# The last expert layer of a four-layer tower: all experts over all tokens, or chosen pairs gathered into blocks

## The chip, the core and the metric

The kernel runs on one core of one Trainium2 chip. The metric is the device time of one execution in microseconds. Engines are named as in the profile: PE (TensorE), PEld (its weight loads), DVE (VectorE), ACT (ScalarE), POOL (GpSimd), SP (SyncE, which here only issues DMAs). "SPq" or "ACTq" rows are DMA issues.

## The reference, cut to what matters

The program is a language-model tower of four layers over 2 x 1024 tokens of width 128, in float32. Each layer is an attention part and a feed-forward part, each behind a layernorm and added to h. Two of the feed-forward parts are mixtures of experts that pick two experts per token: the one of layer 1 (8 experts, hidden width 512) and the one of layer 3 (16 experts of hidden width 96, and a shared one that every token passes). Layer 3's is

```python
g = jnp.clip(h[..., ::2], -gate_clamp, gate_clamp)
u = jnp.clip(h[..., 1::2], -up_clamp, up_clamp)
swiglu5 = g * jax.nn.sigmoid(g * alpha) * gate_scale * (u + up_shift)
...
h = xf @ shared_w1 + shared_b1
z = swiglu5(h, *shared_act) @ shared_w2 + shared_b2
w, idx = jax.lax.top_k(softmax(xf @ gate_w + gate_b), 2)      # w is then divided by its sum
cw = sum over the two of one_hot(idx, 16) * w
he = einsum('nd,edh->enh', xf, expert_w1) + expert_b1
oe = einsum('enh,ehd->end', swiglu5(he, *expert_act[e]), expert_w2) + expert_b2
y = einsum('ne,end->nd', cw, oe)                              # y + z is added to h
```

All but two of the 16 weights in a row of `cw` are zero, so an expert's result counts only for the tokens that picked it.

## The kernel before

The stages run one after another, each in one or more blocks; at a block's end all engines meet. `h` stays in SBUF as 16 tiles of 128 tokens. In a block the order on each engine is written out by hand, and semaphores join the engines. An opening block of a stage, one that only issues loads, holds all engines until SP has issued them.

**Layer 1's heads** (`l1_heads`, attention) keep PE, ACT, DVE and POOL at work; SP has nothing to do there.

**Layer 1's experts** (`stage_l1_ffn`, `slots`, `l1_experts`) already work on chosen pairs. An opening block clears a scratch tensor in DRAM for each batch row (`rows_dram`, 23 blocks of 128 rows each) and loads all second weights `w2_all` (2 MB) and small tables, `b1_all` among them. Two layernorms and the router follow. `slots` counts, for each expert, the tokens that picked it, rounds each count up to whole blocks of 128, and gives each pair of token and pick a slot, and each block an owner (its expert). In `l1_experts`, POOL scatters the rows of the 16 token tiles, twice for two picks, to their slots with indirect DMAs of 64 KB. For each block SP reads the owner into a register and loads its first weights (`load`), and loads the block's rows (`rows`); PE turns the rows, ACT copies them, PE, DVE, ACT and PE do the two products, and ACT issues the store of the results to DRAM. POOL gathers them back when a batch row is complete, and `combine` adds them to `h` by their shares on DVE. The 16 gathers of the second batch row stand behind everything.

**Layer 3's experts** (`stage_l3_ffn`, `l3_expert_scalars`, `l3_experts`) run every expert over every token: 17 experts times 4 units of 512 tokens make 68 units. For a unit PE makes gate and up (`up`), ACT copies each with its bias (`fetch`), DVE limits each (`clip`, L2472), ACT takes the sigmoid, POOL multiplies twice (L2456, L2458), PE makes the second product (`down`, L2388), and DVE adds it to `h` by the token's weight for this expert (`add`, L2482), which is zero for most. The loop over experts is a real loop with two experts a turn.

Of the kernel before, what the change touches and what calls it, by code (L numbers as in the profile page):

```python
# [12 lines left out]
F32 = mybir.dt.float32  # L13
I32 = mybir.dt.int32
# [4 lines left out]
P = 128  # L19
# [101 lines left out]
def layernorm(nc, m, name, src, dst, dstT, gain=None, shift=None, loaded=None):  # L121

    with ExitStack() as ctx:
# [397 lines left out]
def stage_l1_attn(nc, m, w):  # L521
    layernorm(nc, m, "ln_l1a", m.h, m.xn, m.xnT)
    with ExitStack() as ctx:
# [11 lines left out]
        l1_heads(nc, m, r)  # L535
# [126 lines left out]
def l1_heads(nc, m, r):  # L662
# [4 lines left out]
    with ExitStack() as ctx:  # L667
# [23 lines left out]
        block = ctx.enter_context(nc.Block())  # L691

# [412 lines left out]
def l1_experts(nc, m, r):  # L1105
# [5 lines left out]
    with ExitStack() as ctx:  # L1111
# [59 lines left out]
        def _(pool):  # L1171
# [19 lines left out]
            pool.wait_ge(r.w2_in, 48)  # L1191
# [17 lines left out]
        def _(pe):  # L1209
# [31 lines left out]
            pe.wait_ge(r.w2_in, 48)  # L1241
# [99 lines left out]
def stage_l1_ffn(nc, m, w):  # L1341
    with ExitStack() as ctx:
# [3 lines left out]
        r = Core()  # L1346
# [4 lines left out]
        r.b_r, r.ln_g, r.ln_b = sb("b_r", [1, 8]), sb("ln_g", [P, 1]), sb("ln_b", [P, 1])  # L1351
        r.b2_dram, r.b1_dram, r.W1_dram, r.W2_dram = w["L1_ffn_b2"], w["L1_ffn_b1"], w["L1_ffn_W1"], w["L1_ffn_W2"]
        r.s_router, r.n_router = signals(nc, m, "l1f_")("router"), 48
        r.rows_dram = [nc.dram_tensor(f"l1f_rows{b}", (L1_BLOCKS * P, D), F32).ap() for b in range(B)]
        r.s_cleared, zeroed = signals(nc, m, "l1f_")("cleared"), signals(nc, m, "l1f_")("zeroed")
        zero = sb("zero", [P, D])
        r.w2_all, r.b1_all, r.b2 = sb("w2_all", [P, 8, 4 * D]), sb("b1_all", [P, 8, 4]), sb("b2", [8, D])
        r.w2_in = signals(nc, m, "l1f_")("w2_in")
        with nc.Block() as block:
            @block.gpsimd  # L1360
            def _(pool):
                pool.memset(zero[:, :], 0.0).then_inc(zeroed, 1)

            @block.sync
            def _(sp):
                sp.dma_start(r.b_r[:, :], row(w["L1_ffn_b_r"])).then_inc(r.s_router, 16)
                sp.dma_start(r.ln_g[:, :], col(w["L1_ffn_ln_g"]), allow_slow_non_contiguous=True).then_inc(r.s_router, 16)
                sp.dma_start(r.ln_b[:, :], col(w["L1_ffn_ln_b"]), allow_slow_non_contiguous=True).then_inc(r.s_router, 16)
                sp.wait_ge(zeroed, 1)
                for b in range(B):  # L1370
# [1309 lines left out]
```

## Time and profile before

| | us |
|---|---|
| median of 3 runs | 1763.08 (1761.98 to 1763.42) |
| the profiled execution | 1766.68, its span 1764.7 |
| layer 1's heads | 134.9 to 421.8 |
| layer 1's experts, first layernorm to last combine | 439.7 to 624.5 |
| layer 3's experts, first layernorm to last add | 1512.9 to 1757.8 |
| its loop, first POOL multiply to last add | 1557.2 to 1757.8 |

Busy shares of the span: PE 79%, DVE 73%, ACT 45%, POOL 47%. The DMA engines move 37.2 MB, most of it in layer 1's experts. A row of a timeline begins with its start and the time from there to the end of the instructions merged in it, in us; in brackets stands how long the engine was idle before, and what ended that. PEclk is the granted clock of TensorE as a share of 2.4 GHz; 0.50 is its lower level, 1.2 GHz.

### The profile page before, as it was taken

Reading aid. Unit: us, or ns where it says so; the run is one execution under the profiler, and the core shown is the slowest. Engines: PE = TensorE matmul, PEld = TensorE weight load, DVE = VectorE, ACT = ScalarE, POOL = GpSimd, SP = SyncE. Lnnn points to the kernel's source line nnn. Section 1 sums busy time; section 2 is a strip of 40 time slices with the busy share of each in tenths; the row PEclk is TensorE's granted clock in tenths of the full one; section 3 lists DMA queues with packets and bytes.
Section 4 is the critical chain, followed back from the end, with each engine's and each line's share of the span. In section 5 each row is a group of like instructions: output and inputs, shape, how many; then the busy total and the mean of one; then the engine's idle time right before and its main releaser. Section 6 shows DMA issues by size and latency. Waiting matters only on the chain. (4 is left out here: it accounts for less than half of the span.)

```text
span 1764.7 us, 30850 instructions
## 1 busy us (share of the span) xinstructions
PE 1386.9 (79%) x10352; PEld 941.4 (53%) x10360; DVE 1282.3 (73%) x2404; ACT 802.9 (45%) x1006; POOL 821.1 (47%) x624
## 2 busy tenths in 40 slices
PE   2775899994369522258999999999999996499997
PEld 1552666663359511144567666666666664355554
DVE  4265465552625459744699999999999994579997
ACT  2232434441125211014566666666766661166664
POOL 2021333230276656212355555555555542169997
PEclk9986999997579865558999999999999998699998
DMA  3000000003158400000000000000000000000000
GB/s 113 1 1 1 2 2 3 2 2 110 15 145 229 122 6 0 0 0 1 1 1 1 0 0 0 0 0 0 0 0 0 0 1 0 6 13 13 11 12 29
DMA packets 45967, 37.20 MB, mean 21 GB/s; under 512 B 11100, under 2 KB 37367, under 8 KB 45623
## 3 DMA queue, kind: packets, MB, share of 16 engines
q1 hardware_dynamic: 36102, 28.28, 5.9%
q0 software_dynamic: 2048, 4.20, 0.8%
q10 hardware_dynamic: 7728, 3.55, 0.7%
q8 instruction: 56, 0.92, 0.2%
q14 instruction: 33, 0.26, 0.1%
HBM read 26.83 MB, written 9.18 MB: 20 GB/s over the span
## 5 line engine op out<-in xcount | busy, mean ns | idle before, releaser
L1914 POOL TENSOR_TENSOR ta_ex<-ta_ex,ta_left 128x1024 f32<-128x1024 f32 x128 | 302.6, 2364 | 317.2 <-ACT ta_left L1867 316.5
L1826 PEld LDWEIGHTS ta_ps_o<-ta_exT,ta_vseq 128*32 128x32 f32 x2048 | 213.2, 110 | 101.9 <-ACT ta_exT L1859 88.2
L1777 PE MATMUL ta_ps_s<-ta_kT,ta_qz 128*128 (+1 forms) x512 | 242.5, 596 | 20.8 <-ACT ta_ex L1855 20.0
L1826 PE MATMUL ta_ps_o<-ta_exT,ta_vseq 128*32 128x128 f32 x2048 | 247.6, 274 | 6.4 <-ACT ta_exT L1859 6.4
L1859 ACT ACTIVATE ta_exT<-ta_ps_t 128x1024 f32<-128x1024 f32 x128 | 131.1, 1024 | 142.4 <-PE ta_ps_t L1806 142.4
L1932 DVE MAX8 ta_top<-ta_ps_s 128x8 f32<-128x1024 f32 x128 | 156.7, 1224 | 46.2 <-PE ta_ps_s L1777 46.0
L1939 DVE MATCH_REPLACE8 ta_left<-ta_top,ta_ps_s 128x1024 f32<-128x1024 f32 x128 | 155.2, 1212 | 0.0
L1944 DVE MAX8 ta_top<-ta_left 128x8 f32<-128x1024 f32 x128 | 154.5, 1207 | 0.0
L1949 DVE MATCH_REPLACE8 ta_left<-ta_top,ta_left 128x1024 f32<-128x1024 f32 x128 | 154.5, 1207 | 0.0
L1855 ACT ACTIVATE ta_ex<-ta_ps_s,ta_ntop 128x1024 f32<-128x1024 f32 x128 | 142.3, 1111 | 23.8 <-DVE ta_left L1939 23.1
L1867 ACT ACTIVATE ta_left<-ta_left,ta_ntop 128x1024 f32<-128x1024 f32 x128 | 147.0, 1149 | 1.4
L1806 PE MATMUL ta_ps_t<-consts,ta_ex 128*128 128x128 f32 x1024 | 137.8, 278 | 0.8 <-POOL ta_ex L1914 0.8
L1777 PEld LDWEIGHTS ta_ps_s<-ta_kT,ta_qz 128*128 128x128 f32 x512 | 87.3, 190 | 88.0 <-issue 74.4
L1806 PEld LDWEIGHTS ta_ps_t<-consts,ta_ex 128*128 128x128 f32 x1024 | 111.6, 141 | 22.0 <-issue 18.6
L946 ACT ACTIVATE l1h_score<-l1h_work 128x2048 f32<-128x2048 f32 (+1 forms) x40 | 68.5, 1711 | 111.3 <-PE l1h_work L820 111.3
L2456 POOL TENSOR_TENSOR l3e_sig<-l3e_gate,l3e_sig 96x512 f32<-96x512 f32 x68 | 98.7, 1452 | 37.3 <-ACT l3e_sig L2434 37.3
L2388 PEld LDWEIGHTS l3e_ps_d<-l3e_w,l3e_te 96*128 96x128 f32 x544 | 67.4, 195 | 62.7 <-issue 58.3
L2472 DVE TENSOR_SCALAR l3e_gate<-l3e_gate,l3f_limit 96x512 f32<-96x512 f32 x68 | 99.1, 1458 | 0.0
L2458 POOL TENSOR_TENSOR l3e_te<-l3e_up,l3e_sig 96x512 f32<-96x512 f32 x68 | 95.7, 1408 | 5.3
L1016 POOL TENSOR_TENSOR l1h_faded<-l1h_qk,l1h_fade 128x256 f32<-128x256 f32 (+1 forms) x80 | 67.1, 878 | 55.0 <-ACT l1h_fade L959 47.4
L2388 PE MATMUL l3e_ps_d<-l3e_w,l3e_te 96*128 96x128 f32 x544 | 80.2, 292 | 7.1 <-POOL l3e_te L2458 4.8
L841 PE MATMUL l1h_y<-l1h_score,l_v 128*32 128x128 f32 (+1 forms) x1536 | 81.8, 330 | 3.4 <-issue 3.4
(563 smaller groups left out, 2511.9 us busy)
## 6 DMA issues: line engine op xcount, KB each, us to landing
l1e_w<-in_L_ffn_W_dram SPq DMA_DIRECT2D x46, 256.0 KB
l1f_rows<-l1f_zero SPq DMA_DIRECT2D x2, 1472.0 KB, 9.3
l1e_x<-l1f_rows SPq DMA_DIRECT2D x46, 64.0 KB
l1e_outs<-l1e_y ACTq DMA_DIRECT2D x46, 64.0 KB
l3e_w<-in_L_ffn_expert_w_dram SPq DMA_DIRECT2D x16, 96.0 KB, 1.9
ids<-in_x_dram SPq DMA_DIRECT2D x1, 1024.0 KB
consts<-in_consts_dram SPq DMA_DIRECT2D x1, 1024.0 KB, 5.5
out_dram<-h SPq DMA_DIRECT2D x1, 1024.0 KB, 6.1
```

Of the source, the lines that this page charges most:

```text
L1777: ins = pe.matmul(ps_s[:, i % 2, half * BANK:(half + 1) * BANK], qz[:, odd, h, :], kT[:, grp, bass.ds(at.key0[i // PAIR] + half * BANK, BA ...
L1806: ins = pe.transpose(ps_t[:, j * P:(j + 1) * P], ex[:, i % 4, j * P:(j + 1) * P], m.ident)
L1826: ins = pe.matmul(ps_o[a:a + 2 * TW, grp * P:(grp + 1) * P], vseq[:, j, h, :], exT[:, i % 2, j, :], start=(j == 0), stop=(j == CH - 1))
L1855: act.activation(ex[:, i % 4, :], ps_s[:, i % 2, :], ACT.Exp, bias=ntop[:, i % 4:i % 4 + 1], scale=SC).then_inc(s_free, 1)
L1859: act.activation(exT[:, i % 2, :, :].rearrange("p j q -> p (j q)"), ps_t[:, :], ACT.Copy).then_inc(exT_in, 1)
L1867: act.activation(left[:, i % 4, :], left[:, i % 4, :], ACT.Exp, bias=ntop[:, i % 4:i % 4 + 1], scale=SC).then_inc(left_exp, 1)
L1914: pool.tensor_tensor(ex[:, i % 4, :], ex[:, i % 4, :], left[:, i % 4, :], ALU.subtract).then_inc(kept, 1)
L1932: dve.max(top[:, i % 2, 0, :], ps_s[:, i % 2, :]).then_inc(max_done[0], 1)
L1939: dve.match_replace(left[:, i % 4, :], top[:, i % 2, 0, :], ps_s[:, i % 2, :], -BIG).then_inc(first_out, 1)
L1944: dve.max(top[:, i % 2, 1, :], left[:, i % 4, :]).then_inc(max_done[1], 1)
L1949: dve.match_replace(left[:, i % 4, :], top[:, i % 2, 1, :], left[:, i % 4, :], -BIG).then_inc(left_ready, 1)
L2388: ins = pe.matmul(ps_d[:, u % 2, t * P:(t + 1) * P], te[:, g, t * P:(t + 1) * P], w2[:, k, :], start=True, stop=True)
```

## The change

Layer 3's experts get the form of layer 1's. `slots` is run for 16 experts and 32 blocks per batch row. `l3_experts` works on pairs of 128-row tiles: 8 pairs for the shared expert, straight from the turned tokens, then 32 pairs of gathered blocks. First and second weights of an expert are packed beforehand into one DRAM tensor, so that a block has one weight load, into one of 16 buffers. The six scalars and two biases of each block's expert come from seven small matmuls with a table of owners (`hot`) into `par`. The limits are now taken on DVE straight from PSUM (one pass that adds the bias and takes the minimum, one in SBUF that takes the maximum; for up the maximum is fused with the product), and POOL keeps one multiply per pair. Hidden buffers are three deep (`LAG`), the row buffers four.

The clearing of both layers' scratch rows, the packing, and layer 1's small tables are issued by SP in the heads' block; `w2_all` and layer 3's tables are issued by SP inside the layernorm's block (`fetch`), and both opening blocks are gone.

```diff
-        l1_heads(nc, m, r)
+        early = [l1_ffn_early(nc, m, w), l3_early(nc, m, w)]
...
+        l1_heads(nc, m, r, issue_early)
...
+        block.sync(early)
...
-        with nc.Block() as block:
-            @block.gpsimd
-            def _(pool):
-                pool.memset(zero[:, :], 0.0).then_inc(zeroed, 1)
...
-        layernorm(nc, m, "ln_l1f", m.h, m.xn, None)
+        layernorm(nc, m, "ln_l1f", m.h, m.xn, None, fetch=fetch)
...
+        slots(nc, m, r, "l3k", L3_E, L3_BLOCKS, r.raw_act[:, 0:L3_E, 1])
...
+    SHARED, PAIRS = TILES // 2, TILES // 2 + B * NB // 2
+    STAGES, LAG = 16, 3
...
+            def load(j):
+                for n in blocks(j):
+                    s, e = n % STAGES, sp.value_load(r.owner[0:1, n // NB, n % NB:n % NB + 1], min_val=0, max_val=E - 1)
+                    if n >= STAGES:
+                        sp.wait_ge(down_ready, SHARED + (n - STAGES) // 2 + 1)
+                    sp.dma_start(packed[:, s, :], m.packed_dram[bass.ds(e, 1), :, :].rearrange("e p f -> p (e f)")).then_inc(staged[s], 16)
+
+            def rows(j):
+                q = j - SHARED
+                b, n = q // (NB // 2), 2 * (q % (NB // 2))
+                if n == 0:
+                    sp.wait_ge(scattered[b], 16 * 2 * CH)
+                if q >= 4:
+                    sp.wait_ge(x_turned, q - 3)
+                sp.dma_start(x[:, q % 4, :, :], r.rows_dram[b][n * P:(n + 2) * P, :].rearrange("(k p) d -> p k d", k=2)).then_inc(x_in[q % 4], 16)
...
+            for j in range(SHARED, PAIRS):
+                if j + 3 < PAIRS:
+                    rows(j + 3)
+                    load(j + 3)
...
+            def swish(j):
+                pool.wait_ge(sig_ready, j + 1)
+                pool.tensor_tensor(sig[:, j % LAG, :, :], gate[:, j % LAG, :, :], sig[:, j % LAG, :, :], ALU.mult).then_inc(t1_ready, 1)
...
+            for j in range(SHARED):
+                if j < 4:
+                    for t, k in jobs[4 * j:4 * j + 4]:
+                        scatter(0, t, k)
+                swish(j)
+            for j in range(SHARED, SHARED + NB // 2):
+                swish(j)
+                for t, k in jobs[3 * (j - SHARED) // 2:3 * (j - SHARED + 1) // 2]:
+                    scatter(1, t, k)
+            for j in range(SHARED + NB // 2, PAIRS):
+                swish(j)
+                i = j - SHARED - NB // 2 - 3
...
+                if i >= 0:
+                    for t, k in jobs[5 * i // 4:5 * (i + 1) // 4]:
+                        gather(0, t, k)
...
+            for j in range(PAIRS):
+                if j + 3 < PAIRS:
+                    up(j + 3)
+                down(j)
+                if SHARED <= j + 4 < PAIRS:
+                    turn(j + 4)
...
+            def keep(j):
+                q = j - SHARED
+                act.wait_ge(down_ready, j + 1)
+                if q >= 4:
+                    act.wait_ge(y_out[q % 4], 16 * (q // 4))
+                act.activation(y[:, q % 4, :, :], ps_d[:, j % 2, 0:2 * P].rearrange("p (k d) -> p k d", k=2), ACT.Copy).then_inc(y_ready, 1)
...
+            for j in range(PAIRS):
+                sigmoid(j)
+                if SHARED <= j + 3 < PAIRS:
+                    flip(j + 3)
+                if j - 1 >= SHARED:
+                    keep(j - 1)
...
+            def clip(j):
+                dve.wait_ge(up_ready, j + 1)
+                if j >= LAG:
+                    dve.wait_ge(t1_ready, j - LAG + 1)
+                    dve.wait_ge(te_ready, j - LAG + 1)
+                for k in range(2):
+                    p = weights(j, k)[2]
+                    h = ps_h[0:L3_I, j % 2, 2 * k * P:(2 * k + 2) * P]
+                    dve.tensor_scalar(gate[:, j % LAG, k, :], h[:, 0:P], p[BG], p[HG], ALU.add, ALU.min)
+                    ins = dve.tensor_scalar(up_[:, j % LAG, k, :], h[:, P:2 * P], p[BU], p[HU], ALU.add, ALU.min)
+                ins.then_inc(raised, 1)
+                dve.wait_ge(raised, j + 1)
+                for k in range(2):
+                    ins = dve.tensor_scalar(gate[:, j % LAG, k, :], gate[:, j % LAG, k, :], weights(j, k)[2][LG], None, ALU.max)
                 ins.then_inc(clipped, 1)
...
+            def hidden(j):
+                dve.wait_ge(t1_ready, j + 1)
+                if j >= LAG:
+                    dve.wait_ge(down_ready, j - LAG + 1)
+                for k in range(2):
+                    ins = dve.scalar_tensor_tensor(te[:, j % LAG, k, :], up_[:, j % LAG, k, :], weights(j, k)[2][LU], sig[:, j % LAG, k, :],
+                                                   ALU.max, ALU.mult)
+                ins.then_inc(te_ready, 1)
...
+            for j in range(PAIRS):
+                if j + 2 < PAIRS:
+                    clip(j + 2)
+                hidden(j)
+                if 1 <= j and j - 1 < SHARED:
+                    add(j - 1)
...
+def l3_early(nc, m, w):
...
+    def issue(sp):
+        sp.dma_start(m.packed_dram[:, :, 0:2 * L3_I], w["L3_ffn_expert_w1"]).then_inc(m.s_packed, 16)
+        sp.dma_start(m.packed_dram[:, 0:L3_I, 2 * L3_I:], w["L3_ffn_expert_w2"]).then_inc(m.s_packed, 16)
+        sp.dma_start(m.packed_dram[:, L3_I:P, 2 * L3_I:].rearrange("e p d -> p e d"),
+                     m.zero[0:P - L3_I, :].unsqueeze(1).broadcast_to([P - L3_I, L3_E, D])).then_inc(m.s_packed, 16)
+        for b in range(B):
+            sp.dma_start(m.l3_rows_dram[b].rearrange("(n p) d -> p n d", p=P),
+                         m.zero[:, :].unsqueeze(1).broadcast_to([P, L3_BLOCKS, D])).then_inc(m.s_l3clear, 16)
```

## Rows read from the trace of the kernel before

**Rows 1.** The page's first line.
```profile
span 1764.7 us, 30850 instructions
```

**Rows 2.** Chain of work that ended last, 1400 to 1765 us, by line.
```profile
by line: POOL l3e_sig L2456 27.0%; issue 26.3%; POOL l3e_te L2458 3.8%; PE l3e_ps_d L2388 0.6%; POOLq L2455 0.6%; POOLq L2322 0.4%; DVE h L2482 0.2%; POOLq L2460 0.2%; POOLq L2457 0.1%; DVEq L2322 0.1%; DVEq L2479 0.0%; POOLq L2266 0.0%
```

**Rows 3.** Groups by shape, 1557 to 1755 us: busy us, mean ns, idle before.
```profile
L2456 POOL TENSOR_TENSOR l3e_sig<-l3e_gate,l3e_sig 96x512 f32<-96x512 f32 x68 | 98.7, 1452 | 37.3 <-ACT l3e_sig L2434 37.3
L2472 DVE TENSOR_SCALAR l3e_gate<-l3e_gate,l3f_limit 96x512 f32<-96x512 f32 x67 | 98.6, 1471 | 0.0
L2458 POOL TENSOR_TENSOR l3e_te<-l3e_up,l3e_sig 96x512 f32<-96x512 f32 x68 | 95.7, 1408 | 5.3
...
L2472 DVE TENSOR_SCALAR l3e_up<-l3e_up,l3f_limit 96x512 f32<-96x512 f32 x67 | 36.9, 550 | 3.5 <-ACT l3e_up L2428 3.4
```

**Rows 4.** Timeline, entry of the first expert layer: start, duration in us.
```profile
433.62 5.63 SPq L1376 DMA_DIRECT2D l1f_b_all<-in_L_ffn_b_dram  x1
439.68 1.64 DVE L138 BATCH_NORM_STATS2 ln_l1f_stats<-h 128x6 f32<-128x128 f32 x8 [17.89 <-PEq L1359]
```

**Rows 5.** Timeline, entries of three later blocks.
```profile
1471.23 1.64 DVE L138 BATCH_NORM_STATS2 ln_l3a_stats<-h 128x6 f32<-128x128 f32 x8 [1.15 <-PEq L47]
...
1512.94 1.64 DVE L138 BATCH_NORM_STATS2 ln_l3f_stats<-h 128x6 f32<-128x128 f32 x8 [3.15 <-PEq L2247]
...
1541.79 1.28 ACT L2436 ACT_TABLE_LOAD   x1 [1.19 <-PEq L2266]
```

**Rows 6.** Timeline, first layer: start of slots, start of experts, DVE.
```profile
474.35 0.29 DVE L2558 TENSOR_TENSOR l1s_kept<-l1f_picks 128x128 f32<-128x128 f32 x1 [0.54 <-PEq L1034]
...
481.14 2.29 DVE L1318 TENSOR_TENSOR h<-h,xn 128x2048 f32<-128x2048 f32 x1 [0.30 <-PEq L2513]
```

**Rows 7.** Timeline, first layer: sixteenth scatter, first gathered rows turned.
```profile
502.56 0.96 POOL L1173 DMA_INDIRECT l1f_rows<-l1f_hn,l1f_slot  x1 [0.30 <-issue]
...
506.65 0.98 PE L1214 MATMUL l1e_ps_x<-consts,l1e_x 128*128 128x128 f32 x2 [17.32 <-DMA l1e_x<-l1f_rows]
```

**Rows 8.** SP: timeline of first weight loads; waits, 510 to 590 us.
```profile
482.52 2.61 SPq L1151 DMA_DIRECT2D l1e_w<-in_L_ffn_W_dram  x3
...
SPq L1151 <- PE l1e_ps_u L1222: 9.7, 27, 0.8
```

**Rows 9.** Stretches: us, busy PE, PEld, DVE, ACT, POOL, PEclk, DMA share, GB/s.
```profile
424.00:442.00 18.00, 0.00 (x0) 0.00 (x0) 2.25 (x14) 0.00 (x0) 0.00 (x0) 0.50 0.98 281
512.00:540.00 28.00, 28.00 (x254) 28.00 (x253) 14.46 (x30) 14.68 (x30) 24.52 (x44) 1.00 0.85 230
...
720.00:900.00 180.00, 121.46 (x515) 76.38 (x515) 118.01 (x184) 62.17 (x84) 54.45 (x31) 0.75 0.00 1
160.00:190.00 30.00, 25.25 (x352) 15.85 (x356) 17.09 (x24) 8.76 (x12) 11.88 (x14) 0.77 0.01 2
```

**Rows 10.** Groups by shape, first expert layer, 510 to 560 us.
```profile
L1302 DVE TENSOR_TENSOR l1e_pre<-l1e_ps_u,l1e_b 128x512 f32<-128x512 f32 x27 | 18.6, 690 | 38.7 <-PE l1e_ps_u L1222 38.7
...
L1267 ACT ACTIVATE l1e_xT<-l1e_ps_x,l1f_ln_b,l1f_ln_g 128x128 f32<-128x128 f32 x26 | 11.5, 442 | 0.0
...
L1309 DVE COPY l1e_y<-l1e_ps_d 128x128 f32<-128x128 f32 x25 | 7.3, 293 | 5.1 <-PE l1e_ps_d L1232 3.3 <-issue 1.8
```

**Rows 11.** One line's instructions: min/median/max ns.
```profile
L1016 POOL TENSOR_TENSOR l1h_faded<-l1h_qk,l1h_fade x80: 716/732/1717, 148.1 to 378.0; 128x256 f32<-128x256 f32 x64, 128x512 f32<-128x512 f32 x16
```

**Rows 12.** Timeline, last loop: four DVE operations that read PSUM.
```profile
1737.75 1.11 DVE L2482 SCALAR_TENSOR_TENSOR h<-l3e_ps_d,l3f_gates,h 128x128 f32<-128x128 f32 x4
```

**Rows 13.** Timeline, first layer: up matmuls of one block, full clock.
```profile
512.52 1.06 PE L1222 MATMUL l1e_ps_u<-l1e_xT,l1e_w 128*128 128x128 f32 x8
```

**Rows 14.** Timeline, first layer's tail: last stores, last combine.
```profile
597.06 2.59 ACTq L1277 DMA_DIRECT2D l1e_outs<-l1e_y  x3
...
623.01 1.51 DVE L1314 SCALAR_TENSOR_TENSOR h<-l1e_back,l1f_share,h 128x128 f32<-128x128 f32 x4 [3.57 <-DMA l1e_back<-l1e_outs,l1f_slot]
```

**Rows 15.** Timeline, last add of the last layer.
```profile
1756.70 1.13 DVE L2482 SCALAR_TENSOR_TENSOR h<-l3e_ps_d,l3f_gates,h 128x128 f32<-128x128 f32 x4 [1.43 <-PE l3e_ps_d L2388]
```

More of the change, by code:

```diff
@@ L162, in _ @@
                 pool.tensor_tensor(rstd[:, of], small[:, 4, of], m.neghalf[:, of], ALU.pow).then_inc(rstd_ready, 1)
+        if fetch is not None:
+            block.sync(fetch)
         if dstT is None:
@@ new lines, in l3_experts, with blocks, weights @@
+        gates_turned, gates_in, bias_ready, bias_added, h_step = (
+            sem(k) for k in ("gates_turned", "gates_in", "bias_ready", "bias_added", "h_step"))
+        block = ctx.enter_context(nc.Block())
+        def blocks(j):
+            return [2 * (j - SHARED) + k for k in range(2)]
+        def weights(j, k):
+            n = B * NB if j < SHARED else blocks(j)[k]
+            scalars = [par[:, x, n:n + 1] for x in range(7)]
+            if j < SHARED:
+                return w1_all[:, :], w2_all[:, :], scalars
+            return packed[:, n % STAGES, 0:2 * L3_I], packed[0:L3_I, n % STAGES, 2 * L3_I:], scalars
@@ new lines, in up @@
+            def up(j):
+                q = j - SHARED
+                if j == 0:
+                    pe.wait_ge(shared_in, 32)
+                if q >= 0:
+                    pe.wait_ge(xT_ready, q + 1)
+                if j >= 2:
+                    pe.wait_ge(raised, j - 1)
+                for k in range(2):
+                    if q >= 0:
+                        n = blocks(j)[k]
+                        pe.wait_ge(staged[n % STAGES], 16 * (n // STAGES + 1))
+                    rows = r.hT[:, (2 * j + k) * P:(2 * j + k + 1) * P] if q < 0 else xT[:, q % 2, k * P:(k + 1) * P]
+                    for kind in range(2):
+                        ins = pe.matmul(ps_h[0:L3_I, j % 2, (2 * k + kind) * P:(2 * k + kind + 1) * P], weights(j, k)[0][:, kind::2], rows,
+                                        start=True, stop=True)
+                ins.then_inc(up_ready, 1)
@@ new lines, in down @@
+            def down(j):
+                pe.wait_ge(te_ready, j + 1)
+                if 2 <= j < SHARED + 2:
+                    pe.wait_ge(shared_added, j - 1)
+                elif j >= 2:
+                    pe.wait_ge(y_ready, j - 1 - SHARED)
+                for k in range(2):
+                    ins = pe.matmul(ps_d[:, j % 2, k * P:(k + 1) * P], te[:, j % LAG, k, :], weights(j, k)[1], start=True, stop=True)
+                ins.then_inc(down_ready, 1)
+            tables = [r.raw_b1[:, 0::2], r.raw_b1[:, 1::2]] + [r.wide[:, c, :] for c in range(5)]
@@ new lines, in combine @@
+            def combine(b, t):
+                hh = m.h[:, b * CH + t, :]
+                for k in range(2):
+                    dve.scalar_tensor_tensor(hh, back[:, b, t, k, :], r.share[:, k, b * CH + t:b * CH + t + 1], hh,
+                                             ALU.mult, ALU.add).then_inc(h_step, 1)
+                    dve.wait_ge(h_step, 2 * (b * CH + t) + k + 1)
+            dve.tensor_copy(mine[:, 0:B * NB], r.owner[0:G, :, :].rearrange("g b n -> g (b n)"))
+            dve.memset(mine[:, B * NB:], float(E)).then_inc(hot_step, 1)
```

393 lines of the change are left out of this document (195 added, 198 removed).

## The prediction

> **What bounds the kernel now.** The profiled execution spans 1764.7 us [rows 1] and took 1766.68 us; the three plain runs have a median of 1763.08 us, 3.6 us less. The sum below is made in the span of this execution and carried over to the median as a difference. Anything within 0.2% (3.5 us) counts as no change: that is about what a measurement here can tell.
>
> I read first the chain of work that ended last. Over the last 365 us POOL's two multiplies in the last expert loop are by far its largest lines, with "issue" beside them [rows 2]. Then the groups of that loop, kept by shape: 68 units of 512 tokens, and POOL spends 1.45 and 1.41 us on each, 2.9 us a unit, almost without idle time [rows 3]. So the last layer runs all 16 experts and the shared one over all tokens at POOL's pace, and POOL is what the change relieves. Third, the timeline where each stage starts, for idle time that belongs to no engine: before the layernorm of the first expert layer DVE stands still for 17.89 us, while SP issues a table in an opening block [rows 4]; at the last layer it is 3.15 us, and where a layernorm has no such block ahead of it 1.15 us [rows 5].
>
> **Opening blocks.** The slow table and the clearing go under the heads, and the 2 MB of second weights go beside the layernorm. The gap of 17.89 us should fall to 1.15: -16.7 us. At the last layer 3.15 falls to 1.15: -2.0 us. The heads last from 134.9 to 421.8 us (table above); SP has nothing else to issue in them, and they move almost no data. What is moved there: 2.9 MB and 4.2 MB of clearing, 1.6 MB and 0.8 MB of packed weights and their zero tail, together some 10 MB. At the 281 GB/s of the clearing of before [rows 9] this is 35 us of full DMA engines; nothing in the heads waits for a transfer of theirs, so I count 0 and keep up to +5 us for code that is fetched late. The weights that are fetched beside the layernorm start as early relative to their use as before. POOL's first use of them is behind 16 scatters of about 20 us [rows 7], so they are covered.
>
> **Router, scalars, slots.** Two more copies of picks and a broadcast copy of 17x576 add about 1.2 us (128x512 on DVE is 0.69 us [rows 10]). The slots block is new here. For 8 experts it takes 6.8 us from its first DVE instruction to the first one behind it [rows 6]. With 16 experts the tiles are twice as wide and the owner table has 32 blocks: 1024 instead of 368 columns. DVE grows from 0.29 us at 128 columns to 0.69 at 512 [rows 10], so 0.13 us per 128 columns: some fifteen steps of +0.13 to +0.4, two owner steps of +0.7 each and a new scaling step of 0.7 give +4.5. I take 11.3 us; the bounds are 8 and 14. Nothing overlaps it.
>
> **Experts: until the first routed pair.** Before, the block starts at 1541.5 (ACT's table load is 0.3 us into it [rows 5]). In the changed block POOL issues 16 scatters in four groups with a multiply between. In the first expert layer the sixteenth goes out 21.4 us after the start of the block (481.14 to 502.56), and the first transposition of gathered rows comes 4.1 us behind it [rows 6, 7]. Here three multiplies of 96x256 stand between (0.73 us each for this width [rows 11]), and the first of them waits about 5 us for the parameter matmuls, the turned gates and the first pair, all at a cold TensorE. That makes 21.4 + 2.2 + 5 + 4.1 = 33 us, with PE at iteration 4 of 40. The remaining 35 iterations run at a period P.
>
> **The period P.** There are 40 pairs of 256 rows where there were 68 units of 512, so POOL's multiply is now one of 0.73 us per pair. Resource by resource, for a routed pair: POOL has 0.73 plus 1.5 scatters or 1.25 gathers of about 1.2 us: 2.3 to 2.6 us, for 11 and 13 of the pairs.
>
> SP: in the first layer one weight load and one row load take a period less the wait. The period is 1.87 us (254 PE records in 28 us, 17 a block [rows 9]) and the wait 9.7/27 = 0.36 us [rows 8], so 1.5 us; a load alone with its register read is 1.1 us (three in 2.61 [rows 8]). A pair has two loads and one row load: 2.65 us, softened by a lead of some 8 us.
>
> DMA: 328 KB of weights, 131 of rows, 131 of results and 80 to 98 of scatter or gather, some 680 KB. At the 230 GB/s of the first layer (share 0.85) this is 2.95 us, at 281 GB/s (share 0.98) 2.4 us [rows 9].
>
> DVE: four reads of PSUM (four in 1.11 us [rows 12]), two maxima, two products and one wait for itself: 2.3 us. ACT: two sigmoids, a flip, a copy of the result (0.44 us or less each [rows 10]) and a DMA issue: 2.0 us.
>
> Latency: the products of pair j release down (0.6), turn (0.3), flip (0.4), up (1.1 [rows 13]), the clip of pair j+4 (1.75), then the products of pair j+2 (0.55), with 0.5 of semaphores between. That is 5.2 us for two pairs, so 2.6 at the full clock. The PE part, 2.0 us, doubles at the lower level: 3.6.
>
> A pair has 14 PE records of 0.11 us, half of P. Stretches in which PE is busy 67 to 84% of the time show a granted clock of 0.75 to 0.77, a mixture of 1.2 and 2.4 GHz [rows 9]. So I expect a mixture here too, and take P = 3.0 us, between 2.6 and 3.7. The block then lasts 33 + 35 x 3.0 = 138 us to the last down.
>
> **The tail.** The last 16 gathers can only start when the last result is stored. In the first layer it is 24.9 us from the last store's issue (597.06 + 2.59) to the end of the last combine (623.01 + 1.51) [rows 14]. One copy and one issue go ahead: 25.9 us. Before, the last add ends at 1757.8 [rows 15] and the store of h follows in both.
>
> **The sum.** Experts before: 1757.8 - 1541.5 = 216.3 us. After: 138 + 25.9 = 163.9, so -52.4. Slots +11.3, router and scalars +1.2, the last entry -2.0: -41.9 for the last layer. With -16.7 at the first layer: -58.6 us. The span would be 1706.1, the median 1763.1 - 58.6 = 1704.5 us.
>
> The Trainium skill speaks against small transfers: "DMA: Bandwidth & Descriptors", section "Measured (HBM→SBUF, 128 partitions, SWDGE, issued from GpSimd)", says to batch to 1 MiB, as those under 64 KB are dominated by descriptors. By its fit of 2 us plus bytes over 436 GB/s the transfers of a pair, if each stood alone, would come to some 12 us, an estimate from that page by which the kernel would be slower. The trace disagrees: four transfers a block overlap in 1.87 us in the first layer, and what is left of that rule's chance is in the slow rival below.
>
> **Rivals.** *A faster period*, 2.6 us: the full clock holds as in the first layer (1.00 [rows 9]) and the DMA engines give 265 GB/s. Against it: SP at 2.65, DMA at a share of 0.93. 33 + 91 = 124 us: 1690 us. Chance 0.17.
>
> *DVE and POOL hold each other up.* Before, the same clip takes 0.55 us as up and 1.47 us as gate, which starts behind POOL's second multiply [rows 3]. If here each maximum and each product waits for a whole multiply (0.73 us twice in the loop of two pairs), P grows by 0.7 to 3.7: 33 + 130 = 163 us, 1729 us. For it: [rows 3]; against it: the multiply is half as long, and the products wait for it anyway. Chance 0.17. The Trainium skill ("SBUF — State Buffer", section "Who interferes with whom") has this as a lock on a port pair, taken by tensor_scalar in a two-port mode, and by two SBUF inputs against a GpSimd read. By that rule the products would be held too.
>
> *Slower than before.* The pairs hardly overlap: buffers three deep, with scatters ahead of multiplies in POOL's queue, so that a pair passes in turn through turn, flip, up, clip, sigmoid, multiply, products, down and copy, some 7 us. It decides from P = 3.0 + 58.6/35 = 4.7 us on; at 5 us the time is 1775 us. Against it: no resource above comes near that. Chance 0.05.
>
> *The early transfers cost the heads what they save*, the 17 us coming back there: 1721 us. Chance 0.05, as no PE or ACT wait of the heads is for a DMA.
>
> The forecast has 0.56: 1704.5, its own range 1692 to 1718.
>
> **Range and chances.** The fast case and the port case bound it: 1685 to 1730 us. Faster by over 0.2% is all but the slow rival: 0.94; within 0.2% 0.01; slower 0.05.
>
> **What would show it.** The idle time of DVE before the first expert layer's layernorm at about 1.2 us. The slots block of the last layer at 11 us. From the start of the last experts block to the first turned rows 33 us, with POOL's scatters filling it. In the routed part a down every 3.0 us, with PE below 0.9 clock; if the clock is 1.00, P should be nearer 2.6. A SP that waits for PE there, not PE for loads. The last part without PE 26 us long. The prediction is wrong if PE waits for staged weights or rows in most pairs, if the maxima take over 0.9 us in the median, or if the heads grow by more than 5 us.

## The result

The changed kernel takes 1707.4 us in the median (1699.9 to 1708.3, 4 runs) against 1762.5 for the kernel before (1762.0 to 1763.4, 4 runs): a ratio of 0.968, interval 0.966 to 0.970, 55 us less. The forecast was 1704.5, in a range of 1685 to 1730. The same kernel run again (first experiment) gave 1704.1 (1700.4 to 1705.9). The profile shown here is of the execution of 1699.9 us, some 7 us faster than the median; what goes with that spread stands at the end.

The page's first line for the kernel after (against [rows 1]):

```profile
span 1698.2 us, 29060 instructions
```

**The stations.** Timeline of the kernel after: entry of the first expert layer ([rows 4] before), entry of the last ([rows 5]), start of slots ([rows 6] for 8 experts), first and sixteenth scatter, first issue of rows, first turned rows, last down, last combine ([rows 14, 15]):

```profile
418.59 1.65 DVE L141 BATCH_NORM_STATS2 ln_l1f_stats<-h 128x6 f32<-128x128 f32 x8 [0.32 <-PEq L679]
...
1487.62 1.65 DVE L141 BATCH_NORM_STATS2 ln_l3f_stats<-h 128x6 f32<-128x128 f32 x8 [0.32 <-PEq L2144]
...
1518.93 0.43 DVE L2662 TENSOR_TENSOR l3k_kept<-l3f_picks 128x256 f32<-128x256 f32 x1 [0.30 <-PEq L2264]
...
1531.11 1.09 POOL L2392 DMA_INDIRECT l3f_rows<-xn,l3f_slot  x1 [11.63 <-POOLq L2617]
...
1559.80 0.96 POOL L2392 DMA_INDIRECT l3f_rows<-xn,l3f_slot  x1 [0.31 <-issue]
...
1562.06 1.92 SPq L2373 DMA_DIRECT2D l3e_x<-l3f_rows  x4
...
1566.97 0.64 PE L2436 MATMUL l3e_ps_x<-consts,l3e_x 128*128 128x128 f32 x2
...
1663.14 1.22 PE L2464 MATMUL l3e_ps_d<-l3e_packed,l3e_te 96*128 96x128 f32 x4 [2.03 <-DVE l3e_te L2565]
...
1688.87 1.51 DVE L2579 SCALAR_TENSOR_TENSOR h<-l3e_back,l3f_share,h 128x128 f32<-128x128 f32 x4 [3.53 <-DMA l3e_back<-l3e_outs,l3f_slot]
```

The first expert layer starts 21.1 us sooner. The last one is cut into the parts of the prediction: slots 11.5 us (1518.9 to 1530.4), from there to the first turned rows 36.5, the routed part 97.4 us for 35 turns of the loop, 2.78 each, and 26.0 from the last down's end (1664.36) to the last combine's (1690.38).

**The stretches** of the heads' start and of the routed part (columns as in [rows 9]: us, busy PE, PEld, DVE, ACT, POOL, granted clock, DMA share, GB/s):

```profile
135.00:160.00 25.00, 10.62 (x68) 5.33 (x69) 12.33 (x25) 6.60 (x10) 7.03 (x10) 0.76 0.91 247
160.00:190.00 30.00, 23.82 (x344) 15.43 (x344) 17.74 (x27) 8.75 (x12) 12.85 (x14) 0.80 0.42 124
...
1580.00:1600.00 20.00, 14.69 (x103) 11.76 (x104) 18.41 (x62) 9.85 (x30) 15.49 (x18) 1.00 0.83 234
1600.00:1620.00 20.00, 15.78 (x111) 12.41 (x110) 17.99 (x60) 10.90 (x32) 9.12 (x12) 1.00 0.73 201
1620.00:1640.00 20.00, 14.79 (x98) 11.04 (x97) 16.51 (x57) 9.07 (x27) 10.03 (x12) 1.00 0.78 214
```

The DMA engines are full under the start of the heads, where they were idle before, and PE's work there is hardly slower (from 160 to 190 us 23.8 us busy at a clock of 0.80, against 25.3 at 0.77 in [rows 9]). In the routed part nobody is full: DVE 83 to 92%, PE 73 to 79%, DMA 73 to 83% of the time, and the clock is at its upper level throughout. POOL, the bound before [rows 2, 3], is at about half.

**Who is late** in the routed part. SP, whose issues only say when it is free, repeats itself every 2.7 us where nothing holds it (over the whole part its row issues lie 2.6 to 3.6 us apart, but for one wait between the batch rows); it waits 1.8 us for PE in the 103 us from 1562 on:

```profile
1613.79 1.44 SPq L2364 DMA_DIRECT2D l3e_packed<-l3f_packed  x2
1615.27 0.44 SPq L2373 DMA_DIRECT2D l3e_x<-l3f_rows  x1
1616.52 1.44 SPq L2364 DMA_DIRECT2D l3e_packed<-l3f_packed  x2
1617.99 0.44 SPq L2373 DMA_DIRECT2D l3e_x<-l3f_rows  x1
```

And the chain of work that ended last, 1580 to 1655 us, by line (L2361 is the register read, L2364 the weight load, L2373 the rows), is spread over three engines:

```profile
by line: issue 15.0%; SPq L2361 11.6%; SPq L2364 10.7%; PE l3e_ps_h L2453 9.2%; DMA l3e_packed<-l3f_packed 7.9%; DVE l3e_gate L2552 6.2%; PE l3e_ps_d L2464 6.1%; DVE l3e_up L2553 5.7%; SPq L2373 5.5%; DVE l3e_te L2565 4.7%; DVE l3e_gate L25
```

SP's three lines and the transfer behind them make 36% of it, DVE's named lines 17%, PE's 15%. So three theories stood at the start of the experiments: SP's issuing sets the period, DVE does, or the DMA engines do.

### The profile page after: what moved, and what is told of

Same layout as the page of the kernel before. It is cut to its first block and busy times, and to the rows that moved or that the text cites. A ratio compares the mean times of both kernels' runs of the same rounds, so it can differ in the third digit from the quotient of the medians.

```text
span 1698.2 us, 29060 instructions
## 1 busy us (share of the span) xinstructions
PE 1275.9 (75%) x10098; PEld 908.1 (53%) x10106; DVE 1208.3 (71%) x2392; ACT 717.1 (42%) x946; POOL 722.8 (43%) x596
## 5 line engine op out<-in xcount | busy, mean ns | idle before, releaser
L1008 POOL TENSOR_SCALAR_AFFINE_SELECT l1h_decay<-l1h_decay 128x1024 f32<-128x1024 f32 x16 | 17.5, 1092 | 134.9 <-ACT l1h_decay L990 134.9
L1316 DVE TENSOR_TENSOR l1e_pre<-l1e_ps_u,l1e_b 128x512 f32<-128x512 f32 x46 | 31.8, 691 | 51.2 <-PE l1e_ps_u L1236 47.6
L833 PE MATMUL l1h_work<-l1h_faded 32*128 32x256 f32 (+1 forms) x1024 | 60.7, 369 | 3.5 <-POOL l1h_faded L1029 2.2
L1446 PE MATMUL l_ps_t<-consts,l_o 128*128 128x128 f32 x16 | 4.4, 432 | 75.7 <-DVE l_o L1571 75.7
L854 PEld LDWEIGHTS l1h_y<-l1h_score,l_v 128*32 128x32 f32 x1536 | 43.7, 110 | 32.3 <-issue 19.5
```

Of the source, the lines that this page charges most:

```text
L854: ins = pe.matmul(yps[lanes, z // 2, (z % 2) * 2 * P + to.start:(z % 2) * 2 * P + to.stop], keys, score[:, job % RING, head, at], start=(k ...
```

## The experiments

All times are medians of four runs; "down to down" is the median distance, in the profiled execution, between the starts of successive downs (PE, ps_d) where the granted clock of the 5 us around both was 0.99 or more, from the timeline; "block" is from the first scatter to the end of the last combine.

| run | median us (range) | profiled | mean clock | down to down | block |
|---|---|---|---|---|---|
| changed kernel | 1707.4 (1699.9 to 1708.3) | 1699.9 | 0.877 | 2.66 | 159.3 |
| e0 changed again | 1704.1 (1700.4 to 1705.9) | 1700.4 | 0.877 | 2.66 | 160.1 |
| e3 no lower gate limit | 1703.5 (1702.6 to 1707.0) | 1704.0 | 0.871 | 2.36 | 161.4 |
| e4 fixed owner | 1699.4 (1697.6 to 1701.0) | 1697.6 | 0.874 | 2.54 | 154.1 |
| e5 both | 1691.9 (1689.1 to 1698.1) | 1689.1 | 0.874 | 2.26 | 148.8 |
| e1 openings only | 1749.9 (1747.2 to 1750.6) | 1749.8 | 0.883 | | |
| e2 layer 3's setup late | 1714.0 (1712.6 to 1714.6) | 1712.6 | 0.864 | 2.66 | 161.9 |
| e6 weights 7 ahead | 1746.4 (1743.5 to 1748.0) | 1747.3 | 0.837 | (hardly any at 0.99) | 202.4 |
| e7 eight scatters first | 1703.5 (1702.7 to 1714.5) | 1703.2 | 0.874 | 2.71 | 162.6 |
| e8 four shared behind | 1705.2 (1702.3 to 1708.2) | 1706.2 | 0.870 | 2.70 | 161.8 |
| e9 bias in the limits | 1704.2 (1702.5 to 1707.5) | 1704.7 | 0.870 | 2.57 | 160.7 |
| e10 weights 5 ahead | 1709.1 (1703.7 to 1711.9) | 1709.5 | 0.871 | 2.66 | 165.7 |
| e11 three together | 1709.5 (1703.6 to 1711.8) | 1703.6 | 0.872 | 2.73 | 163.5 |

The kernel before gave 1762.1, 1762.0 and 1762.9 beside the three groups (e0, e3 to e5; e1, e2, e6, e7; e8 to e11).

### SP, DVE or DMA: e0, e3, e4, e5

The changed kernel again, without an edit: 

> The changed kernel once more, unaltered, as the reference of the three runs beside it. Its median was 1707.4 us, its profiled execution 1699.9. If the 7 us between these are an accident of one execution, the profiled one lies near 1707 this time; in the routed part a pair every 2.78 us.

No lower gate limit:

```diff
-                dve.wait_ge(raised, j + 1)
-                for k in range(2):
-                    ins = dve.tensor_scalar(gate[:, j % LAG, k, :], gate[:, j % LAG, k, :], weights(j, k)[2][LG], None, ALU.max)
-                ins.then_inc(clipped, 1)
...
-                act.wait_ge(clipped, j + 1)
+                act.wait_ge(raised, j + 1)
```

> Leaves out the gate's lower limit: the two maxima of a pair and DVE's wait for itself ahead of them, so the output is that without this limit. DVE has about 0.8 us less work in a pair (0.3 + 0.48 us). Theory 'SP sets the pace' (0.43 us for the rows and 1.1 for each of two weight loads with their register read, 2.7 us a pair in the stretches without waits): the period stays at 2.65 to 2.78, the time falls by 0 to 4 us. Rival 'DVE sets the pace' (busy 80 to 92% there): the period falls to 2.3 to 2.4, the time by 13 to 17 us. Rival 'the chain through turn, up, clip, sigmoid, multiply, products' sets it: it gets 0.8 us shorter for two pairs, -0.4 us a pair, -14 us.

Fixed owner:

```diff
-                    s, e = n % STAGES, sp.value_load(r.owner[0:1, n // NB, n % NB:n % NB + 1], min_val=0, max_val=E - 1)
+                    s, e = n % STAGES, n % E
```

> Every block's weights are those of the expert with its number modulo 16, a constant, so SP reads no register and computes no address; bytes and the number of transfers are the same, the output is of wrong experts for most blocks. SP then needs about 1.3 us a pair. Theory 'SP sets the pace': the period falls from 2.78 to DVE's 2.5, the time by 7 to 12 us, and PE no longer waits for staged weights. Rival 'DMA sets the pace' (busy share 0.71 to 0.83): no change, within 3 us. Rival 'DVE sets the pace': no change either, but then without the lower gate limit the time falls.

Both edits in one kernel: 

> Both edits together: constant experts, and no lower gate limit. If SP and DVE are two bounds close to each other (2.7 and 2.5 us), this falls by clearly more than the two alone together: a period of 2.2 to 2.4, -14 to -20 us. If DMA is the bound (some 680 KB a pair at 195 to 234 GB/s are 2.9 to 3.5 us), it stays at 2.7. What is left as the bound should be the chain of a pair or POOL (0.73 and up to 1.5 scatters of 1.2).

Against e0's 1704.1, on the same chip: -0.7, -4.7 and -12.2 us. The first lies within the spread of e0's own runs, the second at its edge, the third clear of it. Neither edit alone gives its whole worth, both together give more than the sum: two bounds close to each other. DMA falls as the bound, since e4 and e5 move the same bytes in the same transfers, and e4 moves them faster (237 GB/s from 1580 to 1650 us, 216 in e0). The down-to-down distances say how close: 2.66 with both bounds, 2.54 when only SP is freed, and then the chain (same view as above, e4) is DVE's:

```profile
by line: DVE l3e_gate L2552 18.3%; DVE l3e_up L2553 16.4%; DVE l3e_te L2565 14.8%; PE l3e_ps_h L2453 12.0%; issue 11.2%; PE l3e_ps_d L2464 8.6%; DVE l3e_gate L2557 8.5%; ACT l3e_xT L2508 3.2%; PE l3e_ps_x L2436 3.2%; DVEq L2548 1.1%; ACT l3
```

With both freed (e5) it is PE's (65% of it) and ACT's flip (12%), and the PE timeline of e5 shows a third bound right behind:

```profile
1605.43 0.61 PE L2464 MATMUL l3e_ps_d<-l3e_packed,l3e_te 96*128 96x128 f32 x4
1605.88 0.39 PE L2436 MATMUL l3e_ps_x<-consts,l3e_x 128*128 128x128 f32 x2
1606.73 1.12 PE L2453 MATMUL l3e_ps_h<-l3e_xT,l3e_packed 128*96 128x128 f32 x8 [0.47 <-ACT l3e_xT L2508]
1607.69 0.50 PE L2464 MATMUL l3e_ps_d<-l3e_packed,l3e_te 96*128 96x128 f32 x3
```

PE's own order: down, turn, 0.47 us idle until ACT has flipped what was just turned, up, down: 2.26 us from down to down. Over half of e5's distances at the full clock are exactly this, and none is shorter: it is the floor of that loop.

Why e3 gained nothing although its pairs ran at 2.36: SP still needs 2.7, so PE uses up the lead of staged weights and then waits (4.9 us in five waits). PE timeline of e3:

```profile
1628.11 0.68 PE L2453 MATMUL l3e_ps_h<-l3e_xT,l3e_packed 128*96 128x128 f32 x4 [0.47 <-ACT l3e_xT L2508]
1630.77 0.99 PE L2453 MATMUL l3e_ps_h<-l3e_xT,l3e_packed 128*96 128x128 f32 x4 [1.98 <-DMA l3e_packed<-l3f_packed]
1631.56 1.06 PE L2464 MATMUL l3e_ps_d<-l3e_packed,l3e_te 96*128 96x128 f32 x4
...
1635.33 1.06 PE L2464 MATMUL l3e_ps_d<-l3e_packed,l3e_te 96*128 96x128 f32 x4
```

After the wait of 1.98 us the same four matmuls of down take 1.06 us, not 0.61: the clock is at its lower level, and the next down comes 3.77 us later. So one late transfer costs its own 2 us and then over 1 us on each of the following pairs, until the clock is up again at 1644 us. The start cost e3 something too: its clock was at the lower level until 1578 us, that of the changed kernel until 1567.

### The early part: e1 and e2

e1 is the kernel before with `early = [l1_ffn_early(nc, m, w)]` under the heads and a `fetch` for layer 3's tables, and the old experts' loop. 

> The kernel before with only the first part of the change: layer 1's small tables and scratch clearing go out under its heads, the second weights beside the layernorm, and layer 3's tables beside its layernorm; its experts are the old loop. The prediction priced this at -16.7 and -2.0, 1744 us. The trace of the changed kernel had the first expert layer 21.1 us earlier, of which 3 to 4 lay in the heads. If those come from this edit, 1740 or less; if they are an accident of the clock, 1744. The rival in which the early transfers cost the heads what they save gives 1760.

1749.9: -12.1 us (ratio 0.993, interval 0.991 to 0.994), less than either number. In the profiles, 1749.8 against 1766.7, it is -16.9, and the stations tell it apart:

| station | e1 against the kernel before, us |
|---|---|
| layernorm of the first expert layer (418.58) | -21.1 |
| layernorm of layer 2's attention (607.65) | -21.2 |
| end of that attention's first projections | -18.8 |
| layernorm of the last expert layer (1491.69) | -21.25 |
| end of the span | -17.8 |

Of the -21.1, -17.6 is the gap (17.89 to 0.32) and -3.5 lies in the heads, where the clock of 190 to 220 us is 1.00 and was 0.94. The heads' 3.5 us are not the edit's for certain: the kernel before was 4 us slower in its profiled execution than in its plain ones. Some 6 us come back, in two places, both times with TensorE at its lower clock. At the entry of layer 2's attention the first eight projection matmuls take 5.12 us (2.82 before). In the last layer the router's matmuls take 7.01 us (5.88 before), and from layernorm to POOL's first multiply it is 48.4 us (44.2 before), which gives 3.4 us back. The second gap, 3.15 us to 0.32, is within the -21.25. In the changed kernel's profiled execution only the router's loss is there, not the one at layer 2, so what the openings are worth also hangs on where the clock stands. The plain runs stand: with the old loop behind them the openings are worth 12 us, not 18.7, and the rest of the change 42 to 46.

e2 moves one line, `late = l3_early(nc, m, w)`, into the `fetch` of layer 3's layernorm. 

> The changed kernel with layer 3's packing and clearing (6.6 MB) issued by SP beside layer 3's own layernorm and no longer under layer 1's heads. At 247 to 281 GB/s it takes 24 to 27 us from 1489 us on and ends near 1515, 16 us ahead of the first scatter at 1531, so it should be covered: 1704 to 1707, no change. If its place under the heads mattered (the layernorm, router or tables of layer 3 wait for these transfers), the slots block starts late by up to 20 us: 1710 to 1727.

1714.0: 7 to 10 us above the two medians of the changed kernel. The transfers were in time, the issuing was not. Timeline of e2, SP and PE:

```profile
1494.49 5.58 SPq L2740 DMA_DIRECT2D l3f_packed<-l1f_zero  x1
...
1500.11 7.60 SPq L2743 DMA_DIRECT2D l3f_rows<-l1f_zero  x2
...
1508.16 1.19 PE L1063 MATMUL l3r_ps_l<-l3f_b_r,consts 1*128 1x256 f32 x2 [9.53 <-PEq L126]
```

SP is busy with three issues until 1507.7, the layernorm's block ends only when SP has ended, and the router's first matmul waits 9.53 us where it waits 0.93 in the changed kernel: 8.6 us. (The rest of e2's 12.7 us in the profiles is a start of the routed pairs at the lower clock, which lasted until 1588 us, and 1.3 us ahead of the layer.) So a short block's price is not the transfer's landing, but the issue.

How long an issue takes is not the transfer's own affair either. The table of [rows 4] took SP 5.63 us behind the clearing and the 2 MB of weights. In the changed kernel the same table is issued ahead of the clearing, and the first weights of layer 3 behind it; in e2 those weights have only small tables ahead of them. SP, the changed kernel, then e2:

```profile
136.74 0.38 SPq L2710 DMA_DIRECT2D l1f_b_all<-in_L_ffn_b_dram  x1
...
142.93 5.27 SPq L2736 DMA_DIRECT2D l3f_packed<-in_L_ffn_expert_w_dram  x1
```

```profile
1492.13 0.67 SPq L2738 DMA_DIRECT2D l3f_packed<-in_L_ffn_expert_w_dram  x1
```

Both transfers are short to issue with little ahead of them and take over 5 us behind megabytes, so the issue seems to wait for what was issued before it. Whether another order within the old opening block would have been enough was not run.

### Attempts at a better kernel: e6 to e11

Weights further ahead: `load(j + 7)`, and in e10 `load(j + 5)`, for `load(j + 3)`; rows stay at `j + 3`. 

> The changed kernel with SP's weight loads seven pairs ahead, not three, in the same 16 buffers: SP issues four more pairs' loads while it waits for the scatters, 11 us of its own time. SP needs 2.72 us a pair to DVE's 2.5, so it loses 0.2 us a pair, 7 us over all of them, and the lead holds that. If SP's pace is what cost the 4.7 us that the fixed owners gave back, this gives back the same with the right weights: 1699 to 1700, a period of 2.6. If it was not the pace but the interference of its register reads and address work, or the order of the transfers, nothing changes: 1704.

> The changed kernel with the weight loads five pairs ahead. At seven ahead SP's load had to wait for the pair just ended, and the rows of four pairs ahead were issued behind that wait: PE waited 33 us for rows in 100 us. At five ahead the wait is for the pair three before, so the rows go out in time, and the lead of two more pairs (5.4 us) holds most of what SP loses against DVE. If that explanation of the slow run holds, this is no slower than the changed kernel, and if SP's pace is one of the two bounds, 2 to 5 us faster: 1699 to 1702. If the weights' transfers crowd out the rows' whatever the waits are, it lies between 1704 and 1746.

e6: 1746.4 us, 39 to 42 us slower than the two medians of the changed kernel. Its waits, 1580 to 1680 us (us in total, times, longest):

```profile
PEld l3e_ps_x L2437 <- DMA l3e_x<-l3f_rows: 18.0, 11, 2.4
PE l3e_ps_x L2437 <- DMA l3e_x<-l3f_rows: 15.0, 11, 2.2
```

PE does not wait for weights now but for rows. `load(j + 7)` waits for the buffer of `down(j - 1)`, and in SP's queue `rows(j + 4)` stands behind it. From the down's end it takes SP 1.9 us to have issued two loads and the rows (1611.11 to 1613.04), and the rows 2.4 us to land (the median of their transfers): over 4 us, and the turn is due at the next down. Each such wait also puts the clock down: 0.50 in most of 1590 to 1700. (The 33 us that the expectation of e10 names add the rows of PE and PEld, 15.0 and 18.0, which are the same waits seen twice.)

e10: 1709.1 (1703.7 to 1711.9), no gain; it lies 2 to 5 us above the changed kernel's medians, less than its own spread. Nearly all of e6's loss is gone, as the reading of e6 has it. But the down-to-down distance stays at 2.66, because the rows too come out of SP's queue, at SP's pace, and their lead is still three pairs. Once a row block was late, the clock fell (PE timeline of e10):

```profile
1633.63 0.71 PE L2465 MATMUL l3e_ps_d<-l3e_packed,l3e_te 96*128 96x128 f32 x4
1635.66 0.69 PE L2437 MATMUL l3e_ps_x<-consts,l3e_x 128*128 128x128 f32 x2 [1.32 <-DMA l3e_x<-l3f_rows]
1636.82 2.02 PE L2454 MATMUL l3e_ps_h<-l3e_xT,l3e_packed 128*96 128x128 f32 x8 [0.47 <-ACT l3e_xT L2509]
```

Eight scatters first, `jobs[(0, 8, 12)[j]:(8, 12, 16)[j]]`: 

> The changed kernel with POOL's first 16 scatters as 8, 4, 4 with the shared pairs' multiplies behind each group, not 4, 4, 4, 4. Four scatters of 1.26 us fall into the 4.9 us that POOL waits for the first sigmoid. The last of the 16 should go out 5 us sooner, the rows be turned at about 1562, not 1567: -3 to -5 us, 1699 to 1704. If down and clip of the shared pairs, not the scatters, set when the turning starts, 0 to -1.

1703.5 (up to 1714.5, that run at a mean clock of 0.857): no gain. DVE's first clip, ready to start when PE's first up ended at 1538.0, came at

```profile
1542.40 0.41 DVE L2552 TENSOR_SCALAR l3e_gate<-l3e_ps_h,l3e_par 96x128 f32<-96x128 f32 x1 [8.10 <-remote]
```

behind something that the trace can't name, 4 us late, and POOL waited 4.15 us again. Whether that is DVE's code arriving late behind POOL's transfers stays open.

Shared pairs 4 to 7 behind the routed ones (e8): in `l3_experts` `SHARED = 4`, `LAST = SHARED + B * NB // 2`, the first scatters in groups of 4, 6 and 6, POOL's tail

```diff
+            swish(LAST)
             for k in range(4):
                 pool.wait_ge(y_out[k], 16 * 2 * NB // 8)
-            for t, k in jobs:
+            for j in range(LAST + 1, PAIRS):
+                for t, k in jobs[2 * (j - LAST - 1):2 * (j - LAST)]:
+                    gather(1, t, k)
+                swish(j)
+            for t, k in jobs[6:]:
                 gather(1, t, k)
```

and the first row's combines between the late adds. 

> The changed kernel with four of the eight shared pairs moved from ahead of the routed pairs to behind them, under the 16 last gathers (a multiply behind every second gather), and the first batch row's combines beside them. The last result is then stored four pairs sooner, -10 us, and POOL's queue of gathers gets three multiplies of 0.85 us and the last combines more work from DVE, +3. The first gathered rows are turned behind fewer pairs, as soon as the 16 scatters have landed: 1557 to 1560. Sum -5 to -9 us against the changed kernel's 1704: 1695 to 1699. Rival: DVE has 24 us of work behind the last routed pair and becomes the end of the tail, or the start gets slower as the shared pairs no longer cover the scatters: 1704 or more.

1705.2, no gain, and the block of the profiled execution is 161.8 us, not 5 to 9 us below the 159.3 of the changed kernel. The scatters had covered five shared pairs before; now PE has one, and waits. PE timeline of e8:

```profile
1564.78 0.69 PE L2450 MATMUL l3e_ps_x<-consts,l3e_x 128*128 128x128 f32 x2 [9.53 <-DMA l3e_x<-l3f_rows]
...
1567.76 1.06 PE L2478 MATMUL l3e_ps_d<-l3e_w_all,l3e_te 96*128 96x128 f32 x4
1568.61 0.64 PE L2450 MATMUL l3e_ps_x<-consts,l3e_x 128*128 128x128 f32 x2
1569.72 2.02 PE L2467 MATMUL l3e_ps_h<-l3e_xT,l3e_packed 128*96 128x128 f32 x8 [0.47 <-ACT l3e_xT L2522]
1571.53 1.06 PE L2478 MATMUL l3e_ps_d<-l3e_w_all,l3e_te 96*128 96x128 f32 x4
```

Behind 9.53 us of idle PE the clock is at its lower level, and PE's order takes 3.77 us a pair (1571.53 - 1567.76), five times on end. The first rows were turned 30.0 us behind the first scatter, 5.9 sooner than in the changed kernel (35.9); five pairs at over 1 us more each took that back. The tail did what it should: 25.3 us of gathers and combines (1671.26 to the end of the last combine, 1696.60) with the shared pairs beside them.

The bias in the limits: DVE `tensor_scalar(gate, h, p[HB], p[LB], ALU.min, ALU.max)`, ACT `Sigmoid(bias=p[AB])` and `Identity(bias=p[BG])`. 

> The changed kernel with the gate's bias taken out of both limits beforehand, so that one pass of DVE from PSUM limits it on both sides; ACT adds the bias inside the sigmoid and in two more passes of 0.38 us. DVE has 0.6 us less work a pair, ACT 0.75 more (busy 50% before). As with the lower limit left out, nothing is gained alone if SP's 2.7 us a pair is the next bound: 1702 to 1704. If it falls by 5 or more, DVE was the bound and the earlier run was wrong about it.

1704.2: as with e3, nothing alone; down to down 2.57.

> The three edits of the runs beside it in one kernel: four shared pairs behind, the bias in the limits, weights five ahead. With both bounds of the routed pairs relieved the period should be the 2.5 us or less that the fixed owners without a lower limit gave (-12 us), and the late shared pairs add their -5 to -9: 1684 to 1688 us. If ACT's two passes or the chain of a pair take the bound's place, the period stays at 2.7 and 1695 is left.

1709.5 (1703.6 to 1711.8), 21 to 26 us above what was expected. PE's weight loads wait for rows here (4.9 us in seven times, longest 1.7, 1580 to 1650), the start is that of e8 (clock 0.50 from 1562 to 1580), down to down is 2.73. e8 and e10 each brought waits of PE, and none of the three edits takes work from SP; that this is why they add up to nothing is argued, not tested. None of the versions that keep the whole computation beats the changed kernel by more than its spread.

## Why the prediction was right, step by step

**What bounds the kernel before** held as far as the runs go: POOL's two multiplies fill the old loop [rows 3], and the last layer lost 42 to 46 us with the new one (e1 to the changed kernel, medians). The new loop also has far fewer rows to work on, 40 pairs of 256 instead of 68 units of 512, and no run takes only POOL's work away, so POOL's own share is read from the rows and not tested.

**Opening blocks**, -18.7 us: the mechanism is right (both gaps are 0.32 us, even less than 1.15, 20.4 us less together; the heads show no loss beside 247 GB/s), the size was off: 12.1 us in plain runs. The failed step is that time saved ahead of a layer is saved whole; the traces of e1 show some 6 us given back by a colder TensorE, at layer 2's attention and in the last layer. The words "slow table" are wrong too: its issue takes 0.38 us where nothing large is ahead of it. And e2 shows that even well-covered transfers cost 7 to 10 us if SP issues them in a short block.

**Router, scalars, slots**: forecast 11.3 for slots, 11.5 measured. The router's matmuls were 1.1 us longer, for the clock.

**Until the first routed pair**, 33 us forecast, 36.5 measured. The scatters were sized right: 28.6 us from the block's start to the sixteenth, of which 5 for the first sigmoid; measured 29.4 (1530.4 to 1559.80), with a wait of 4.89. The failed term is the last, 4.1 us from there to the turned rows, taken from a layer where the turn waits for nothing else: it was 7.2. SP issued the rows at 1562.06, but the first turn stands in PE's queue behind the fifth shared down, and that was late because POOL's multiplies had waited among the scatters.

**The period**, 3.0 forecast, 2.78 measured (2.66 at the full clock). Two of the terms were close: SP 2.65 (about 2.7 measured where nothing holds it), DVE 2.3 (2.54 when it alone decides, e4). Two failed. *Latency*: with SP and DVE out of the way (e5) it is not a chain over two pairs of 5.2 us that binds but PE's own order, 2.26 us for one pair at the upper level and 3.77 at the lower. The sums of 2.6 and 3.6 were near by luck. *The clock*: a mixture was expected, with PE busy half the time and by the likeness to the stretches of [rows 9]; in the profiled execution PE was busy 66 to 79% of the time, much as there, and the clock was 1.00 from 1580 to 1656 us. Where it fell in the routed parts of these profiles, PE had been idle just before. Of the signs that were named, SP waiting for PE failed too: it did so for 1.8 us in 103.

**The tail**: 25.9 forecast, 26.0 measured.

**The rivals.** *A faster period* of 2.6 us came nearest of them: the full clock held in the profiled execution, which took 1699.9 us, but DMA gave 195 to 234 GB/s and not 265, and did not have to give more. *DVE and POOL hold each other up*: not in the routed part, where the products take 330 to 343 ns each (54 of 54, 1580 to 1655 us) and the maxima 281 ns in the median, 529 at most. But the effect is there. In the stretch with shared pairs the two products take 1.07 us, not 0.60, when POOL's multiply starts just ahead of them (one product of the two takes 0.81 us then):

```profile
1570.94 0.75 POOL L2401 TENSOR_TENSOR l3e_sig<-l3e_gate,l3e_sig 96x256 f32<-96x256 f32 x1 [1.53 <-ACT l3e_sig L2515]
...
1571.02 1.07 DVE L2565 SCALAR_TENSOR_TENSOR l3e_te<-l3e_up,l3e_par,l3e_sig 96x128 f32<-96x128 f32 x2
```

The Trainium skill's rule on this ("SBUF — State Buffer", section "Who interferes with whom"), an exclusive lock of a shared port pair, agrees with these rows; in the routed part no product starts while a multiply of POOL runs, so the order of the loop keeps the two apart. *The pairs hardly overlap*, 1775 us: no. The Trainium skill's rule against small transfers ("DMA: Bandwidth & Descriptors", section "Measured (HBM→SBUF, 128 partitions, SWDGE, issued from GpSimd)"), to batch to 1 MiB or more, did not decide here: the prediction's estimate of 12 us a pair had each transfer alone, and the measured 2.66 us has transfers of 128 and 160 KB that overlap, at 195 to 234 GB/s together.

**Sum.** Opening -12 (forecast -18.7), last layer -42 to -46 (forecast -39.9): a miss of 7 us and one of 3 to 6 with opposite signs. That the total came within 3 us of the forecast is in part luck.

## What to carry to other kernels

When the bound is removed, list the next three resources with their price per turn; here they were 2.7, 2.5 and 2.3 us, so no single further edit could give more than 5 us, and only the run with both edits showed what lay behind. Count the issuing queue as an engine: here a weight load with its address from a register costs SP over a microsecond, and everything that stands behind it in the queue inherits its pace and its waits, and a short block cannot end before its large transfers are issued. In a loop that PE does not fill, a wait of PE of a microsecond or two can take the clock down for the next 7 to 23 us, so spend buffers where PE would stand still, and judge small edits by several runs beside their mean clock.

## What the runs showed of the hardware

- *SP's register read is dear.* With the owner read into a register two weight loads and a row load repeat every 2.7 us; with a constant every 1.5 us where nothing holds SP (e4). That is 0.6 us a load for the read and the address. Rows of e4, SP:

```profile
1614.29 0.94 SPq L2364 DMA_DIRECT2D l3e_packed<-l3f_packed  x2
1615.27 0.43 SPq L2373 DMA_DIRECT2D l3e_x<-l3f_rows  x1
1615.75 1.03 SPq L2364 DMA_DIRECT2D l3e_packed<-l3f_packed  x2
```

- *Idle times of PE of one to two microseconds went before falls to 1.2 GHz, but not always.* The lower level came behind idle times of 1.98 us (e3), 1.37 us (e0), 1.32 us (e10) and 9.53 us (e8), and once behind one of 0.74 us between two of 0.5 (e9). Two of 1.57 us in e3 (1590 and 1596 us) left it at 1.00, as did waits of up to 1.04 us in the profile after; so the length of one wait does not decide it. It then stayed down for 7 us (e0), 12 to 13 (e3, e9) and 23 (e10). At the lower level four matmuls take 1.06 us, not 0.61 to 0.71, and a pair 3.77 us. That fits the spread between runs of one kernel: three of e7's four lie at 1702.7 to 1703.8 us with mean clocks of 0.866 to 0.877, the fourth at 1714.5 with 0.857; the changed kernel's at 1699.9 with 0.877 and at 1706.6 to 1708.3 with 0.866 to 0.871. What makes the difference from run to run was not settled.
- *An issue takes long behind large transfers*: the same table 5.63 us behind a clearing and 0.38 ahead of it, the same 1.5 MB of weights 5.27 us behind a clearing and 0.67 without (e2). The issues of 256 KB for 16 experts' tails and of two clearings of 2 MB took 5.58 and 7.60 us in e2, behind 2.3 MB of weights, and the block could not end before. How much may be queued before the issue waits was not measured.
